# Another order and another engine for the weight splits at the end of the last batch

## The reference

```
x = layernorm(x + attention(x))          # x: 8 batches, 1024 tokens, 256 wide; 16 heads
gates = softmax(x @ gate_w)              # 8 experts, the best 2 of each token
h = gelu(ln(x @ w1[e] + b1[e]) * g + b)  # 256 -> 512
y = h @ w2[e] + b2[e]                    # 512 -> 256
x = layernorm(ln(sum_e weight_e * y_e + x))
```

## Time and profile before

| | us |
|---|---|
| three runs, median | 2425.51 |
| lowest, highest | 2420.11, 2425.64 |
| profiled execution | 2408.44 |
| its span | 2406.7 |

### The profile page before, as it was taken

The page is one execution under the profiler, slowest core; times in us unless marked ns, Lnnn a source line. Parts: engine busy times, 40 slices in busy tenths (PEclk is TensorE's granted clock), DMA queues, the critical chain, the costliest instruction groups (busy, mean ns, idle before and its releaser), DMA issues. The chain is left out here.

```text
span 2406.7 us, 43666 instructions
## 1 busy us (share of the span) xinstructions
PE 2111.4 (88%) x12268; PEld 1473.2 (61%) x12268; DVE 1718.2 (71%) x4997; ACT 1365.9 (57%) x3316; POOL 1302.6 (54%) x1478
## 2 busy tenths in 40 slices
PE   2698899899899899899989989974399999999598
PEld 2455555555556566556555555633299988988487
DVE  3477577678668668768767768825588888888398
ACT  0255555565555565565565556563278777778254
POOL 1545544774665556566475476451677777776000
PEclk7789898999899899999999989995699999999799
DMA  4555655565555645755654656515022222222475
GB/s 125 124 126 136 123 108 141 125 140 127 129 114 117 152 107 116 161 118 116 150 124 110 149 122 136 114 41 201 21 77 74 72 72 74 76 72 65 160 244 170
DMA packets 190519, 284.47 MB, mean 118 GB/s; under 512 B 54072, under 2 KB 111056, under 8 KB 190160
## 3 DMA queue, kind: packets, MB, share of 16 engines
q1 hardware_dynamic: 170832, 237.48, 41.6%
q0 software_dynamic: 17152, 35.81, 4.9%
q10 hardware_dynamic: 2304, 8.39, 0.9%
HBM read 99.48 MB, written 37.90 MB: 57 GB/s over the span
## 5 line engine op out<-in xcount | busy, mean ns | idle before, releaser
L516 ACT ACTIVATE probs<-scores_T 128x512 f32<-128x512 f32 (+3 forms) x1536 | 654.6, 492 | 249.2 <-PE scores_T L406 237.7
L749 POOL TENSOR_SCALAR_AFFINE_SELECT probs<-probs 128x256 f32<-128x256 f32 x512 | 206.1, 411 | 529.1 <-ACT probs L516 526.1
L464 PE MATMUL ring<-k_stack,q_stack_b 96*128 96x512 f32 (+3 forms) x1024 | 398.7, 432 | 21.4 <-DVE neg_part L661 9.5
L661 DVE TENSOR_REDUCE neg_part<-ring 128x1 f32<-128x512 f32 x512 | 333.5, 684 | 97.9 <-PE ring L464 94.8
L406 PE MATMUL scores_T<-q_stack_b,k_stack 98*128 98x512 f32 (+3 forms) x1024 | 321.0, 389 | 46.0 <-ACT probs L516 44.5
L423 PE MATMUL o_ps<-probs,v_ones 128*17 128x512 f32 (+3 forms) x3072 | 344.3, 522 | 1.8 <-POOL probs L749 1.6
L464 PEld LDWEIGHTS ring<-k_stack,q_stack_b 96*128 96x128 f32 x1024 | 194.3, 199 | 228.3 <-issue 80.1
L666 DVE CUSTOM_DVE_ANT_0 ring<-ring,mask 128x384 f32<-128x384 f32 (+3 forms) x512 | 243.6, 507 | 118.8 <-PE ring L464 116.7
L666 DVE CUSTOM_DVE_ANT_0 ring<-ring,mask,neg_part 128x384 f32<-128x384 f32 (+3 forms) x512 | 260.5, 554 | 69.6 <-PE ring L464 68.7
L1063 ACT ACTIVATE o_sb<-ht_ps,ln_b,ln_g 128x128 f32<-128x128 f32 x544 | 217.8, 450 | 93.7 <-PE ht_ps L1012 86.0
L406 PEld LDWEIGHTS scores_T<-q_stack_b,k_stack 98*128 98x128 f32 x1024 | 188.5, 201 | 101.0 <-ACT probs L516 78.9
(11 more groups left out here) (186 smaller groups left out, 4554.8 us busy)
## 6 DMA issues: line engine op xcount, KB each, us to landing
u_rot<-u SPq DMA_DIRECT2D x128, 256.0 KB, 3.7
k_stack<-u_rot SPq DMA_DIRECT2D x128, 256.0 KB
lat_w<-lat_split SPq DMA_DIRECT2D x32, 512.0 KB
q_stack_a<-u_rot SPq DMA_DIRECT2D x64, 256.0 KB
q_stack_b<-u_rot SPq DMA_DIRECT2D x64, 256.0 KB
k_stack<-u SPq DMA_DIRECT2D x64, 256.0 KB
y<-y_rows SPq DMA_DIRECT2D x32, 512.0 KB, 6.3
x_raw<-in_xT SPq DMA_DIRECT2D x16, 512.0 KB, 4.7
```

Of the source, the lines that this page charges most:

```text
L464: nc.tensor.matmul(out[:, 0:k1 - k0], q_stack[qb // 4][0:3 * L, row_buf(n, qb // 4), h, P * (qb % 4):P * (qb % 4) + P], k_stack[0:3 * L, n ...
L516: nc.scalar.activation(probs[:, s % 2, h, cols], sc[(t + j) % 3][:, HALF - w:HALF], ACT.Exp).then_inc(exp_done, 1)
L661: nc.vector.tensor_reduce(neg_part[:, n % 2, part_col], src[:], AX_X, ALU.max, negate=True).then_inc(max_taken, 1)
L749: nc.gpsimd.affine_select(both, both, [[0, 2], [1, P]], ALU.is_ge, zero, base=0, channel_multiplier=-1).then_inc(kept, 1)
```

## The change

The list of items changes in three ways, all in the end block.

VectorE's order becomes: C 0 to 7, the table copies, NX 0 to 7, W0, W1, then G and a split in turn (G0, W2, G1, W3, ... G7, W9), R 0 to 21, the tables, the weights.

The splits W10 to W15 are subtracted on GpSimd instead of VectorE: W10 to W12 between Y and NORM, W13 to W15 between NORM and the scatters. ScalarE's order of high parts, and of loads, becomes `hi_order`: 10, 0, 11, 1, 12, 2, 3, 13 ahead of turn 0, and one of 14, 4, 15, 5, 6, 7, 8, 9 behind each turn.

The place of ZT is one lower in the last batch, so that TensorE's order becomes: turn 0, turn 1, gate product 0, turn 2, gate product 1, and so on.

```diff
--- before.py
+++ after.py
@@ -276,8 +276,11 @@
                 put("RES", ("RES", b))
                 put("ZB", ("ZB", b))
             if g == GROUPS - 1:
-                for name in ("C", "NX", "ZT", "G"):
+                for name in ("C", "NX", "G"):
                     put(name, *[(name, b, tb) for tb in range(TB)])
+                first, pace = PLACES["ZT"]
+                ahead = 1 if b == B - 1 else 0
+                at += [(first - ahead + pace * tb, ("ZT", b, tb)) for tb in range(TB)]
                 put("NORM", ("NORM", b))
                 put("STORE", ("STORE", b))
                 put("R", *[("R", b, i) for i in range(R_STEPS)])
@@ -715,7 +718,7 @@
                         dve.wait_ge(scattered, 16 * 2 * TB * n)
                     route_step(n, i).then_inc(routed, 1)
                 elif kind == "W":
-                    dve.wait_ge(w_hi_ready, n + 1)
+                    dve.wait_ge(w_hi_ready, hi_order.index(n) + 1)
                     w, e = parts[n]
                     lo = experts[w + "_lo"][:, e, :]
                     nc.vector.tensor_tensor(lo, lo.bitcast(F32), experts[w + "_hi"][:, e, :].bitcast(F32),
@@ -762,6 +765,12 @@
                     nc.gpsimd.tensor_scalar(z_ve[:], z_mv[:, :, 1], EPS, None, ALU.add).then_inc(ve_ready, 1)
                     pool.wait_ge(ve_ready, n + 1)
                     nc.gpsimd.tensor_tensor(z_rstd[:], z_ve[:], half[:], ALU.pow).then_inc(rstd_ready, 1)
+                elif kind == "W":
+                    pool.wait_ge(w_hi_ready, hi_order.index(n) + 1)
+                    w, e = parts[n]
+                    lo = experts[w + "_lo"][:, e, :]
+                    nc.gpsimd.tensor_tensor(lo, lo.bitcast(F32), experts[w + "_hi"][:, e, :].bitcast(F32),
+                                            ALU.subtract).then_inc(w_lo2_ready, 1)
                 elif kind == "SCAT":
                     k, tb = it[2:]
                     if k == 0 and tb == 0:
@@ -813,17 +822,22 @@
         w_tmp, w_sum = sb("w_tmp", [P, TILES]), sb("w_sum", [P, TILES])
         parts = [(w, e) for e in range(E) for w in ("w1", "w2")]
         w_loaded = [sem(f"w_loaded{i}") for i in range(len(parts))]
-        w_hi_ready, w_lo_ready = sem("e_hi_ready"), sem("e_lo_ready")
+        w_hi_ready, w_lo_ready, w_lo2_ready = sem("e_hi_ready"), sem("e_lo_ready"), sem("e_lo2_ready")
         end_tables, b_loaded, ln1_loaded = sem("end_tables"), sem("b_loaded"), sem("ln1_loaded")
         b_zeroed, b_split, b_kept = sem("b_zeroed"), sem("b_split"), sem("b_kept")
         table_step, diff_exp, done = sem("table_step"), sem("diff_exp"), sem("route_done")
         table_loads = [(limit, "limit"), (slot_no, "slot_no"), (tile_row, "tile_row"),
                        (base0, "base"), (rows2, "rows2")]
-        scat_at, c_at = [it[0] for it in late].index("SCAT"), [it[0] for it in late].index("C")
-        between = [x for it in late[c_at:scat_at] for x in
-                   ((it, ("W", 2 + it[2] // 2)) if it[0] == "NX" and it[2] % 2 else (it,))]
-        late = [("W", 0), ("W", 1)] + late[:c_at] + between + late[scat_at:]
-        late_weights = [("W", w) for w in range(6, len(parts))]
+        weights = lambda a, b: [("W", w) for w in range(a, b)]
+        zt_at, c_end = late.index(("ZT", B - 1, 0)), late.index(("C", B - 1, TB - 1)) + 1
+        hi_order = (10, 0, 11, 1, 12, 2, 3, 13, 14, 4, 15, 5, 6, 7, 8, 9)
+        g_at = late.index(("G", B - 1, 0))
+        late_act = late[:zt_at] + [("W", w) for w in hi_order[:TB]] + [
+            x for it in late[zt_at:] for x in ((it, ("W", hi_order[TB + it[2]])) if it[0] == "ZT" else (it,))]
+        late_dve = late[c_end:g_at] + weights(0, 2) + [
+            x for it in late[g_at:] for x in ((it, ("W", 2 + it[2])) if it[0] == "G" else (it,))]
+        norm_at, scat_at = late.index(("NORM", B - 1)), late.index(("SCAT", B - 1, 0, 0))
+        late_pool = (late[:norm_at] + weights(10, 13) + late[norm_at:scat_at] + weights(13, len(parts)) + late[scat_at:])
 
         with nc.Block() as block:
             @block.sync
@@ -849,23 +863,24 @@
 
             @block.scalar
             def _(act):
-                for i, (w, e) in enumerate(parts):
+                for i in hi_order:
+                    w, e = parts[i]
                     act.dma_start(experts[w + "_lo"][:, e, :].bitcast(F32), dram[w][:, e, :]).then_inc(w_loaded[i], 16)
-                scalar_items(act, late)
-                scalar_items(act, late_weights)
+                scalar_items(act, late_act)
                 act.wait_ge(routed, R_STEPS * B)
                 nc.scalar.activation(w_tmp[:], routes["weight"][:, 1, :], ACT.Exp).then_inc(diff_exp, 1)
 
             @block.vector
             def _(dve):
                 nc.vector.memset(experts["b2"][:].bitcast(F32), 0.0).then_inc(b_zeroed, 1)
+                vector_items(dve, late[:c_end])
                 dve.wait_ge(end_tables, 16 * len(table_loads))
                 nc.vector.tensor_copy(routes["ones2"][:], rows2[:])
                 dve.wait_ge(b_loaded, 16)
                 nc.vector.tensor_copy(b_hi[:], b_raw[:]).then_inc(b_split, 1)
                 dve.wait_ge(b_split, 1)
                 nc.vector.tensor_tensor(b_lo[:], b_raw[:], b_hi[:].bitcast(F32), ALU.subtract).then_inc(b_split, 1)
-                vector_items(dve, late)
+                vector_items(dve, late_dve)
                 steps = [0]
 
                 def then(ins):
@@ -896,18 +911,18 @@
                 nc.vector.tensor_copy(routes["row"][:], row_f[0:1, :])
                 then(nc.vector.tensor_scalar(expert_f[:], expert_f[:], float(E - 1), None, ALU.min))
                 nc.vector.tensor_copy(routes["expert"][:], expert_f[0:1, :])
-                vector_items(dve, late_weights)
                 dve.wait_ge(diff_exp, 1)
                 then(nc.vector.tensor_scalar(w_sum[:], w_tmp[:], 1.0, None, ALU.add))
                 then(nc.vector.reciprocal(routes["weight"][:, 0, :], w_sum[:]))
                 nc.vector.tensor_tensor(routes["weight"][:, 1, :], routes["weight"][:, 0, :], w_tmp[:],
                                         ALU.mult).then_inc(done, 1)
-                dve.wait_ge(w_lo_ready, len(parts))
+                dve.wait_ge(w_lo_ready, 10)
                 dve.wait_ge(done, 1)
 
             @block.gpsimd
             def _(pool):
-                gpsimd_items(pool, late, None)
+                gpsimd_items(pool, late_pool, None)
+                pool.wait_ge(w_lo2_ready, len(parts) - 10)
                 pool.wait_ge(scattered, 16 * 2 * TILES)
 
     return experts
```

## The result

| | before | after |
|---|---|---|
| median, 20 runs each (us) | 2425.23 | 2408.39 |
| lowest to highest | 2400.94 to 2437.02 | 2399.55 to 2429.84 |
| profiled execution, its span | 2408.44, 2406.7 | 2409.88, 2408.2 |

The ratio of after to before is 0.9946, 95% interval 0.9922 to 0.9969: 13.1 us less (7.5 to 18.9), where 12.4 was forecast. The medians lie 16.8 apart and the means of the twenty (2423.82 and 2409.87) 14.0, both inside that interval.

A forecast was written before the change was run, and what follows sets the result against it. The last batch's end block was taken to add directly to the kernel's time, with GpSimd's scatters finishing last. Scatters 11.3 plus earlier route steps 1.1 gave 12.4 us less: 2425.5 to 2413.1, range 2406 to 2418.

The forecast's parts named there:

- Part 1: Last batch's scatters on GpSimd: with splits 6 to 15 gone from behind VectorE's tables, the seventh falls 12.28 to 0.96, saving 11.32 us.
- Parts 2 to 4: End block: statistics first, 7 to 8.6 us early; GpSimd splits around the roots, 2.35 each; roots done 1648.7, normalizations 1653.7.
- Part 5: VectorE up to the route steps: ten splits 11.4, two GpSimd splits 4.7, logit copies 1.4; start 1671.2 against 1672.30.
- Part 6: TensorE's turns one tile ahead in the gate loop: worth nothing, as its time lies beside VectorE's longer 17.5 us.
- A: Rival on the end block: splits on GpSimd and VectorE don't hinder each other; 19.5 us saved, 2406.0; chance 0.24.
- B: Rival on the seventh scatter: its hole is no wait for VectorE; only 1.1 us won, 2424.4, no change; chance 0.10.
- C: Rival on GpSimd's splits: rounding output makes each cost far more; at 5.9 us a split, 8.9 slower, 2434.4; chance 0.04.

The follow-up runs named there:

- the row sums: Kernel before with splits 6 to 15 on VectorE replaced by one-operand row sums over the same 128x1024 part; block 75.20 and, repeated, 74.87 us against 86.50.
- the last version: Changed kernel with no GpSimd splits, 1 to 7 between logits, 0 and 8 to 15 behind the tables with column copies between; block 62.00 us, ratio to before 0.9876.

## Why the prediction was right

*Part 1, the scatters.* 33.09 to 21.77 forecast, 21.73 measured. The reading (GpSimd waits for VectorE's two-operand splits) was tested from three sides: splits moved, gaps between them, one operand. That it is the second SBUF operand rests on the row sums and on the 12 and 6 scatters of the attention phase. By the Trainium skill (page "SBUF — State Buffer", section "Who interferes with whom") such a `tensor_tensor` takes only the read side of the ports shared with GpSimd and would not stall descriptor generation, which is marked there as inferred. Here the scatter was held up, 12.28 for 0.96, and the measurement decides. The scatter itself reads `slot` and `ids` from SBUF; whether those reads are what waits, as the prediction allowed, or the descriptors, no run separates. That only its beginning waits would fit the reads.

*Parts 2 to 4.* Statistics, roots and last normalization came within 0.3 us of the forecast. Three GpSimd splits ahead of the roots took 7.00 against 7.05; the price taken from `y_T`'s product (2.35) held for the rounding output too. Split 13 came ahead of the first normalization, as forecast.

*Part 5, the one mis-sized term.* Route steps started 1.7 us earlier than forecast, and that is the gap between 12.4 and the block's 14.0. Of it 0.8 is the logit copies: I took 0.17 each, their whole length, but between splits one adds only 0.07 (a split and a copy take 1.21, a split back to back with the next 1.14). 0.5 is GpSimd's two splits, which cost VectorE 3.30 - 1.21 = 2.09 each, not 2.35: GpSimd's first ends at 1673.68, 2.22 after VectorE's split began, and VectorE's ends 1.08 after that, less than its own 1.21. 0.3 is the normalizations' end. Against this stands 0.17 more behind the last scatter, which is within what that tail varies by (3.77 and 3.48 in two runs of the same kernel).

*Part 6 was wrong.* The turns ahead were forecast to be worth nothing, because their loop of 14.6 us lies beside 17.5 us of VectorE. The sums don't decide it: GpSimd's two splits fall on the first tiles, and over the last ones VectorE needs only 1.21 a tile, less than the loop's 2.08. Undone, it costs 1.56 us at the route steps and 1.2 in the block. The forecast time did not suffer from this, since its sum took VectorE as never waiting for the loop, which is true with the edit.

*The rivals.* A (splits don't hinder each other) falls by the run with the roots first and by the 3.30. B falls by the moved splits. C falls by the 7.00 for three.

*The time itself.* The measured median is 4.7 us under the forecast 2413.1. The block accounts for 1.6 of it (14.0 for 12.4); the other 3 are in no row of the block, and the interval of 7.5 to 18.9 leaves room for them as noise.

What the forecast's sum hides is how the gain divides. It credited 11.3 us to the end of the hole. But moving the ten splits ahead of the route steps and nothing else gives 86.9 for 86.5: their 11.4 us move with them. The change pays because six splits go elsewhere and the ones left on VectorE lie where it had waited for the gate loop (2.08 a tile, of which it worked 0.17). The six on GpSimd are the poorer part of it: the version with all sixteen on VectorE is 2.5 us faster.

## What to carry to other kernels

Moving work out of another engine's way is worth only what idle time takes it up; sum the engine's whole list, not the stall alone, and compare rates tile by tile rather than totals. Before sharing elementwise work between VectorE and GpSimd, look in the trace for one pair that overlapped: if one waits out the other there, sharing costs. Where a VectorE run of two-operand work must lie beside GpSimd's DMAs, a wait and a tiny one-operand operation between the pieces let the DMAs through here: the first one held cost 1.1 us, each further one some 0.2 (steps of 1.45 instead of 1.26).

## What the runs showed of the hardware

- The two engines do not give way alike. Ten VectorE splits back to back kept one scatter waiting for all of them (12.28), and two kept a GpSimd split waiting until a logit copy came (4.50 for 2.35). Five GpSimd splits back to back did not keep VectorE's normalizations out: one got in after each.
- What holds a scatter up is a VectorE operation with both operands in SBUF. One that takes an operand from PSUM did not, though it wrote as much (12 scatters at 0.98, against 6 at 1.47 to 1.52). A scatter that began 0.54 or more ahead of such an operation took 1.01 and was held no longer.
- A cast of 128x128 with one SBUF operand also waited for GpSimd's split (2.17, and 0.19 in the last version, with no split there), while a row sum of 128x1024 did not hold a scatter up. And an operation of 128x8 on GpSimd waited for two VectorE splits (4.06 for 1.79).
- One execution ran TensorE far slower in all its phases: 4496.99 us, its matmul group at 759 ns where the same group takes 434 in the repeat (the page's groups, the odd run first), while the mean granted clock in its records is 1.0. Why is open.

```profile
L464 PE MATMUL ring<-k_stack,q_stack_b 96*128 96x512 f32 (+3 forms) x1024 | 710.3, 759 | 0.9 <-DVE neg_part L661 0.5
```

```profile
L464 PE MATMUL ring<-k_stack,q_stack_b 96*128 96x512 f32 (+3 forms) x1024 | 401.1, 434 | 18.8 <-DVE neg_part L661 8.8
```
